# Attention probabilities transposed in 32x32 blocks on the vector engine instead of on the matmul engine, in an adaLN + attention + GRU + FFN kernel

## The reference

```python
# x: (B=128, S=32, E=256); 32 heads of 8 features
y    = adaln(x)                      # block summary attention, then a layer norm per token
q, k, v = split(y @ W_attn + b_attn)         # (128, 32 heads, 32, 8)
scores = einsum('bhqd,bhkd->bhqk', q, k) / sqrt(8)
scores = where(causal, scores, -10000) + alibi
probs  = softmax(scores, axis=-1)            # (128, 32, 32, 32)
attn   = einsum('bhqk,bhkd->bhqd', probs, v)
x      = x + attn @ W_proj + b_proj
h      = GRU over the 32 tokens of x, state (128, 256)   # sequential
out    = x + h @ (weight * scale).T + bias
```

## Time and profile before

| | us |
|---|---|
| median of 3 runs | 445.61 (443.76 to 445.76) |
| the profiled execution, its own time | 445.15 |
| its span, first to last instruction | 443.3 |
| start, up to the first `normalise` | 51.29 |
| attention, first to last `normalise` | 205.76 |
| the rest: last projection, GRU, FFN | 186.25 |

### The profile page before, as it was taken

One profiled execution on the slowest core, in us unless ns is written; L12 is line 12 of the kernel. 1 busy time (PEld: TensorE's weight loads), 2 busy tenths in 40 slices (PEclk: granted clock), 3 DMA queues, 4 the chain that ended last, 5 costly groups with the idle time before them and its releaser, 6 DMA issues.

```text
span 443.3 us, 13432 instructions
## 1 busy us (share of the span) xinstructions
PE 423.8 (96%) x5448; PEld 350.9 (79%) x5448; DVE 326.1 (74%) x995; ACT 236.4 (53%) x553; POOL 93.2 (21%) x114
## 2 busy tenths in 40 slices
PE   8899999999999999999999899999999999999994
PEld 5656687786877878778687698899999999999984
DVE  3587888798888877879777844677776677777665
ACT  7355657566575675755666753444444444444341
POOL 7663142432132221322235500000000000000000
PEclk9999999999999999999999999999999999999999
DMA  7942413223133141231213000001000000000001
GB/s 289 394 183 70 135 40 100 70 61 109 35 90 96 50 120 39 86 95 53 74 33 92 27 1 2 0 2 47 20 31 24 25 24 26 25 24 25 24 25 71
DMA packets 34268, 30.36 MB, mean 68 GB/s; under 512 B 4128, under 2 KB 29344, under 8 KB 34208
## 3 DMA queue, kind: packets, MB, share of 16 engines
q1 hardware_dynamic: 34208, 29.51, 20.5%
HBM read 16.92 MB, written 8.39 MB: 57 GB/s over the span
## 4 chain that ended last, share of the span: by engine, by line
PE 75%; DVE 15%; ACT 4%; issue 3%; POOL 1%; DVEq 0%; ACTq 0%; POOLq 0%
PE ps_a L1267 10%; PE ps_s L1432 7%; PE ps_t L1432 6%; PE ps_o L1432 6%; PE ps_s L1327 6%; PE ps_s L1488 5%; PE ps_t L1488 5%; PE ps_a L1488 4%; PE ps_t L1340 4%; PE ps_m L1371 4%; PE ps_m L1488 4%; PE ps_o L1351 3%; PE ps_m L1363 3%; DVE mx L963 2%; ACT y L599 2%
## 5 line engine op out<-in xcount | busy, mean ns | idle before, releaser
L531 POOL TENSOR_TENSOR sc<-masked,mx 128x512 f32<-128x512 f32 x32 | 45.7, 1429 | 143.3 <-DVE mx L963 143.3
L955 DVE COPY_PREDICATED masked<-kst,ps_s 128x512 f32<-128x512 int32 x64 | 44.1, 736 | 6.1 <-PE ps_s L1327 5.8
L1267 PE MATMUL ps_a<-yT_r,w_qkv_r 128*128 128x512 f32 x180 | 46.0, 403 | 1.3 <-DVE yT_r L936 0.9
L754 ACT ACTIVATE zg<-ps_t,brz 128x128 f32<-128x128 f32 x64 | 20.1, 365 | 39.6 <-PE ps_t L1432 37.3
L963 DVE TENSOR_REDUCE mx<-masked 128x16 f32<-128x512 f32 x64 | 40.5, 674 | 0.0
L1267 PEld LDWEIGHTS ps_a<-yT_r,w_qkv_r 128*128 128x128 f32 x180 | 32.6, 188 | 9.6 <-issue 2.8
L637 ACT ACTIVATE sc<-sc 128x512 f32<-128x512 f32 x64 | 37.3, 621 | 4.2 <-DVE sc L969 2.9
L1101 DVE SCALAR_TENSOR_TENSOR rg<-ps_o,vec,rg 128x128 f32<-128x128 f32 x64 | 19.5, 346 | 24.8 <-PE ps_o L1432 23.8
L570 ACT ACTIVATE pT<-ps_t 128x512 f32<-128x512 f32 x64 | 34.9, 595 | 4.5 <-PE ps_t L1340 3.4
L1327 PE MATMUL ps_s<-kbd,qn 64*32 64x256 f32 x1024 | 36.3, 382 | 0.8 <-issue 0.8
L1432 PEld LDWEIGHTS ps_s<-hT,w_hh 128*128 128x128 f32 x256 | 33.1, 191 | 4.9 <-DVE hT L1119 2.8
(11 more groups left out here) (159 smaller groups left out, 827.2 us busy)
## 6 DMA issues: line engine op xcount, KB each, us to landing
xf<-in_x_feat SPq DMA_DIRECT2D x8, 512.0 KB, 9.5
xg<-in_x_tok SPq DMA_DIRECT2D x8, 512.0 KB, 5.1
kbd<-kn SPq DMA_DIRECT2D x128, 32.0 KB, 1.9
v_dram<-vn SPq DMA_DIRECT2D x16, 256.0 KB, 2.5
vbd<-v_dram SPq DMA_DIRECT2D x64, 64.0 KB, 2.1
out_feat<-ost SPq DMA_DIRECT2D x16, 256.0 KB, 2.0
w_qkv<-in_wqkv SPq DMA_DIRECT2D x1, 768.0 KB, 9.7
w_ih<-in_wih SPq DMA_DIRECT2D x1, 768.0 KB, 13.3
```

Of the source, the lines that this page charges most:

```text
L531: nc.gpsimd.tensor_tensor(shifted, kept, m.unsqueeze(2).to_broadcast([P, NH // 2, S]), ALU.subtract).then_inc(sc_sub[1], 1)
L754: nc.scalar.activation(dst[:, c, :], gate_part(gate, c, t), ACT.Sigmoid, bias=brz[:, b0 + c:b0 + c + 1]).then_inc(done, 1)
L955: nc.vector.copy_predicated(kept, keep.unsqueeze(1).to_broadcast([P, NH // 2, S]), ps_s[:, h * 512:(h + 1) * 512].rearrange("p (h k) -> p ...
L1267: last = nc.tensor.matmul(bank, w_qkv_r[a][:, c, first_col + m * P:first_col + (m + 1) * P], yT_r[b][:, c, :], start=(a == b == c == 0), s ...
```

## The change

The scores of a tile are laid out with head-in-four and query down the partitions, and sequence, head-quad and key along the free dimension. Then every 32x32 block [query x key] can be transposed where it stands, and DVE does so with two instructions of 128x512, SBUF to SBUF. The eight PE transposes and the two ACT copies of a tile are gone. The rest follows from it: 

- `scores` is 32 products of 32 rows and 32 columns of the array with 128 moving columns, where it was 16 of 64 rows with 256; its semaphore rises once per tile, so `softmax_mask` waits for all of a tile's scores. The row of the array and the output quadrant are rotated against each other, `head = (r + c) % HG`.
- `kbd` has two buffers in the same memory (4 key slots in place of 8), 4 DMAs for each half group with twice the bytes each.
- `transpose_probs(n)` moves to DVE, after `softmax_mask(n+1)` and ahead of `softmax_max(n+1)`.
- The residual sum of all tiles but the last goes to POOL, with ACT's `projection_out` in front of it.
- ACT runs `softmax_exp(n)` at the start of step n, on both sides of `attn_out(n-1)`, in place of at the end of step n-1, and `projection_out(n-1)` right behind it, ahead of the copies of keys, queries and values and of `normalise_tokens`.
- On DVE `rest_of_y` goes ahead of `softmax_mask`, `token_stats` behind `softmax_shift`.
- `ps_t`, free now, takes the queries and values; `ps_a` keeps the keys and the transposed tokens.

```diff
-BY_POOL = range(NT - GT, NT - 1)
+BY_POOL = range(NT - 1)
@@ memory
-            kbd = ...nc.sbuf_tensor("kbd", [P, C, KH, GC], F32))
+            kbd = ...nc.sbuf_tensor("kbd", [P, 2, C, KH, GC], F32))
-            pT = ...nc.sbuf_tensor("pT", [P, NQ, P], F32))
+            pT = ...nc.sbuf_tensor("pT", [P, NH * S], F32))
@@ ACT tile_step
+                softmax_exp(n, n % 2, 0)
                 if i == 0 and not last_group:
                     round_y(g + 1, 0)
                     round_y(g + 1, 1)
                 if n > 0:
                     attn_out(n - 1)
-                probs_out(n)
+                softmax_exp(n, n % 2, 1)
+                if n - 1 in BY_POOL:
+                    projection_out(n - 1)
...
-                if n - 1 in BY_POOL:
-                    projection_out(n - 1)
-                if n + 1 < NT:
-                    softmax_exp(n + 1, (n + 1) % 2)
@@ DVE
-                    dve.wait_ge(sc_mm, 2 * n + h + 1)
+                    dve.wait_ge(sc_mm, n + 1)
...
+            def transpose_probs(n, p):
+                dve.wait_ge(pv_mm, n)
+                for h in range(2):
+                    cols = slice(h * 512, (h + 1) * 512)
+                    dve.wait_ge(sc_exp, 2 * n + h + 1)
+                    nc.vector.transpose(pT[:, cols], sc[:, p, cols]).then_inc(pt_out, 1)
@@ DVE tile_step
+                if i == 0 and g + 1 < NG:
+                    rest_of_y(g + 1)
                 if n + 1 < NT:
                     softmax_mask(n + 1, (n + 1) % 2)
-                if i == 0 and g + 1 < NG:
-                    rest_of_y(g + 1)
                 if norm_ahead and i == 2:
                     add_proj(g + 2, ps_a)
...
+                transpose_probs(n, n % 2)
...
-                if norm_ahead and i == 2:
-                    token_stats(g + 2)
                 if n + 1 < NT:
                     softmax_max(n + 1, (n + 1) % 2)
                     softmax_shift(n + 1, (n + 1) % 2)
+                if norm_ahead and i == 2:
+                    token_stats(g + 2)
@@ PE
-                for c in range(C):
-                    for r in range(RH):
-                        rows = slice(r * P // RH, (r + 1) * P // RH)
-                        for b in range(TB):
...
-                            last = nc.tensor.matmul(ps_s[b * S:(b + 1) * S, out_cols], qn[rows, g % 2, c, cols],
-                                                    kbd[rows, c, :, cols], start=True, stop=True,
-                                                    tile_position=(r * P // RH, b * S))
+                for b in range(TB):
+                    cols = slice(i * P + b * S, i * P + (b + 1) * S)
+                    for c in range(C):
+                        out_col = score_column(c * KH, b)
+                        for r in range(HG):
+                            rows, head = slice(r * S, (r + 1) * S), (r + c) % HG
+                            last = nc.tensor.matmul(
+                                ps_s[head * S:(head + 1) * S, out_col:out_col + KH * S], qn[rows, g % 2, c, cols],
+                                kbd[rows, g % 2, c, :, cols], start=True, stop=True,
+                                tile_position=(r * S, head * S))
+                last.then_inc(sc_mm, 1)
@@ PE tile_step
-                transpose_probs(n, n % 2, first=(n == 0))
```

More of the change, by code:

```diff
@@ L26 @@
 HG = 4
-RH = 2
-KH = P // RH // 8
 NQ = NH // HG
-HW = NQ // 2
+KH = NQ // C
 GC = GT * P
@@ L307, in product_bank, with value_bank @@
                     4: ps_s[:, 512:1024], 5: ps_m[:, :]}.get(k, ps_a[:, 0:512])
+        def value_bank(k, h):
+            return (ps_m[:, :], ps_a[:, 0:512])[h] if k == 0 else ps_t[:, h * 512:(h + 1) * 512]
         def block_keys(k):
@@ L378, in load_k @@
                 cols = slice(half * TH * P, (half + 1) * TH * P)
-                for h in range(KH):
-                    sp.dma_start(kbd[h:P:KH, :, h, cols], kn[h:P:KH, :, cols]).then_inc(k_in[half], DMA)
+                for j in range(KH):
+                    sp.dma_start(kbd[j:P:KH, k % 2, :, j, cols], kn[j:P:KH, :, cols]).then_inc(k_in[half], DMA)
             def save_v(k, half):
@@ L556, in _ @@
                         softmax_shift(n + 1)
+                    if i == 2 and g + 2 < NG:
+                        inverse_std(g + 2)
                     if n - 1 in BY_POOL:
@@ L560, in _ @@
                         block_sums(g + EARLY)
-                    if i == 2 and g + 2 < NG:
-                        inverse_std(g + 2)
                     if g == NG - 2 and i > 0:
@@ L610, in q_chunk @@
                 if m == 0 and k >= 2:
-                    act.wait_ge(sc_mm, 2 * GT * (k - 1))
-                nc.scalar.activation(qn[:, k % 2, m, :], ps_a[:, m * GC:(m + 1) * GC], ACT.Identity,
+                    act.wait_ge(sc_mm, GT * (k - 1))
+                nc.scalar.activation(qn[:, k % 2, m, :], ps_t[:, m * GC:(m + 1) * GC], ACT.Identity,
                                      bias=bq[:, m:m + 1], scale=SCALE).then_inc(q_out, 1)
@@ L629, in v_half, with softmax_exp @@
                 nc.scalar.activation(vn[:, half, :, :].rearrange("p h (t w) -> p t h w", t=TH),
-                                     ps_a[:, half * 512:(half + 1) * 512].rearrange("p (t h w) -> p t h w", t=TH, h=HG),
+                                     value_bank(k, half).rearrange("p (t h w) -> p t h w", t=TH, h=HG),
                                      ACT.Identity, scale=key_factor).then_inc(v_out, 1)
[L633 to L644, removed]
+            def softmax_exp(n, p, h):
+                act.wait_ge(sc_sub[h], n + 1)
+                part = sc[:, p, h * 512:(h + 1) * 512]
+                nc.scalar.activation(part, part, ACT.Exp).then_inc(sc_exp, 1)
             def projection_out(n):
@@ L1066, in tile_step @@
                     cond_scores(3)
+                if i == 0 and g in (0, 2):
+                    cond_shift(2 + g // 2)
+                transpose_probs(n, n % 2)
                 if i == 1 and g in (0, 2):
@@ L1075, in tile_step @@
                     softmax_shift(n + 1, (n + 1) % 2)
-                if i == 0 and g in (0, 2):
-                    cond_shift(2 + g // 2)
+                if norm_ahead and i == 2:
+                    token_stats(g + 2)
                 if norm_ahead and i == 2:
@@ L1260, in project_qk @@
             def project_qk(k, first_col, done, m):
-                bank = ps_a[:, m * GC:(m + 1) * GC]
+                bank = (ps_a if done is k_mm else ps_t)[:, m * GC:(m + 1) * GC]
                 for a, b in ((0, 0), (1, 0), (0, 1)):
@@ L1320, in scores, with prob_block @@
                     pe.wait_ge(sc_out, 2 * n)
[L1321 to L1341 removed]
+                for b in range(TB):
[9 more added lines that the diff above has]
+                last.then_inc(sc_mm, 1)
+            def prob_block(q, b):
+                return slice(score_column(q, b), score_column(q, b) + S)
             def probs_v(n, g, i):
@@ L1598, in qk_cols @@
     def qk_cols(w):
-        return w.reshape(-1, RH, C, KH, HD).transpose(0, 2, 1, 4, 3).reshape(-1, E)
+        split = w.reshape(-1, C, KH, HG, HD)
+        rows = [np.roll(split[:, c], -c, axis=2).transpose(0, 2, 3, 1).reshape(-1, P) for c in range(C)]
+        return np.concatenate(rows, 1)
     def v_cols(w):
```

66 lines of the change are left out of this document (29 added, 37 removed).

## The result

The kernel after takes 457.54 us in the median of 4 runs (455.98 to 458.38), the kernel before 445.65 beside it. The ratio is 1.0273, with a 95% interval of 1.0233 to 1.0313: slower, as forecast, but by 12 us where the sum gave 4. The profiled execution took 455.98 us, 10.83 more than that of before.

The account below looks back on a forecast made before the run. PE was taken to limit steps i = 0 and 1, DVE i = 2, i = 3 and three steps of the last group. Terms summed to +4.15 us on 445.15, giving 449.3 us; range 440 to 468.

Parts of the forecast that it names:

- the pace of DVE's transposes: Two DVE transposes per tile: 1.27 us a pair, net +0.60 per step where DVE is the limit.
- the scores' eight parts: PE's scores: eight array parts work at once, 0.8 us plus 0.25 of start-up, costed at nothing.
- the wait for ACT ahead of `project_out`: `project_out` follows `transpose_attn` by 0.90 us, not 1.15, so PE's steps gain 0.25, not 1.05.
- i = 2 and i = 3 as DVE's steps: DVE limits them: i = 2 +0.88 in groups 0 to 5, i = 3 +0.60 in groups 2 to 6.
- POOL's sums hidden: Two residual sums on POOL, about 1.0 us a tile, cost nothing; POOL is busy 1.41 to 2.62 of a step.
- Both transpose rivals: DVE transposes fast, 0.43 us each: 442.0 us, chance 0.20; or slow, 2.6 a pair: 472.1, chance 0.12.
- both scores rivals: Scores four at a time: 465.3 us, chance 0.12; row parts sharing a bank take turns: 497.3, chance 0.04.
- i = 0, "-0.25 - 0.34 + 0.09": Groups 1 to 6: shorter `project_out` wait, keys no longer late, tokens 0.09 later; -0.50 each, -3.0 us in all.
- i = 3 in groups 0 and 1, "PE stays the limit: -0.25": PE's block products of 1.9 us keep PE the limit there; -0.25 each, -0.5 us in all.
- i = 1, -0.25: PE's step gains 0.25 us and nothing else moves; in 7 groups -1.75 us.
- The start, -1.2: First step: `rest_of_y` ahead of the mask, no PE transposes, first scores ahead of half the values; -1.2 us.
- The fourth step's zero: Last group's fourth step: 0.8 us saved by the copy, as much lost by the order; zero.

Follow-up runs that it names:

- the kernel with filler in one step: Kernel after, with PE transposing the identity into free `ps_t`, result unread, in steps i = 3 of groups 0 to 6 alone: 453.43 us, ratio 1.0185.
- the tokens first: Kernel after with ACT's `normalise_tokens` and `cond_out` ahead of `projection_out` for i = 3: 455.36 us, ratio 1.0217.
- the two best kernels: Kernel after with `normalise_tokens` and `cond_out` earlier, both shifts on POOL, idle PE products throughout (442.83 us) or in i = 3 of groups 0 to 6 alone (442.89).

## Why the prediction was right in direction and wrong in size

*Right:* the pace of DVE's transposes; the scores' eight parts; the wait for ACT ahead of `project_out`; i = 2 and i = 3 as DVE's steps (+0.71 and +0.37 a step, forecast 0.88 and 0.60); POOL's sums hidden; the GRU unchanged (186.22 us). Both transpose rivals and both scores rivals are out: four parts writing one bank, in different quadrants, would have taken 3.2 us if they took turns, and took 1.15. The rule that I had from the Trainium skill, TensorEngine Tiling (Array Packing), Gotcha 1, and gave a chance doesn't hold for this use.

*Wrong:* the measured sum is 6.8 us over mine. Of these 2.8 come by the clock; 1.9 by the program's supply (1.2 in one pair of steps, 0.7 in i = 1); 2.3 in the pairs i = 3 and i = 0 that start in groups 0 and 1 (13.86 and 15.20 us, +0.21 and +0.63 where I had -0.75 each); 0.4 in the rest of i = 1; 0.9 at the start; less 1.0 in i = 2 and 0.6 in the last group. What failed most was never written as a term: that PE's own pace stays what it was.

- **The clock.** I priced PE's idle time in i = 3 and in the fourth step of the last group at nothing, since DVE or a chain sets those steps. The granted clock fell there and in the last group: it is slow in the second half of i = 3 and at the start of i = 0 (158 to 162 and 189 to 192 us), and in the fourth step. By the windows: pairs i = 3 and i = 0 at groups 3 to 4 and 4 to 5, 13.92 and 13.56 us where the kernel with filler in one step has 13.03 and 13.01, and the fourth step at 5.40 where 4.03 is had at full clock: 0.89 + 0.55 + 1.37 = 2.8 us.
- **The program's supply.** The pair at groups 2 to 3 holds both stalls: 14.23 us, against 13.03 without them, 1.2. Two more are too short to show as idle time: the scores that start at 199.69 and 228.55 us take 1.43 and 1.49 us, not 1.15, with a halt behind matmuls 3499 and 4130, 12 and 17 times 126.2 past 1984. Their steps i = 1 take 7.60 and 6.97 us, 7.30 and 6.61 with filler in one step: 0.7. Against that, the kernel before has its own stall at groups 5 to 6 (13.49 us for the pair, else 12.7); it is gone after (13.02). That gives 0.6 back by luck, as much as the three other pairs are too long beside clock and supply (0.2 each). Whether the change brings more such stalls because it gives PE twice as many matmuls for the scores is not shown. Filler in one step takes 4.1 us off the median (457.54 to 453.43; 3.9 by the ratios). I can't split that further by medians, as the filler moves the packets too.
- **i = 0, "-0.25 - 0.34 + 0.09".** The arithmetic held: tokens done at 5.56, so scores 0.75 later, at 6.31 us after the start of i = 3; measured at full clock, in the kernel with filler in one step, 4.93 + 1.35 = 6.28. But I added this -0.50 to a +0.60 for i = 3 as if the two were apart. The pair is one chain, bound through ACT; DVE's share of it is free. At full clock it is 13.0, my two terms gave 12.9, and the +0.37 in place of +0.60 for i = 3 is lost again in i = 0. (It is +0.37 since a pair of transposes takes 1.21 us from start to start, not 1.27, and the normalising and the mask ahead of it take 0.13 less than before. In i = 2 the mask starts only 0.08 later, not 0.21.)
- **i = 3 in groups 0 and 1, "PE stays the limit: -0.25".** Two things stood behind. `cond_out`, the copy of the block products, comes after `normalise_tokens` on ACT; its PSUM is what `transpose_y` writes next, and PE stands idle for 0.75 us ahead of that (72.66 and 102.06; the copy ends 0.09 and 0.10 before). With the tokens first that wait is gone, and i = 0 of group 1 takes 7.70, not 8.45 us. And in group 1 DVE scales `w_f` in this step, which I overlooked; DVE's and POOL's timelines after:

```profile
100.87 1.54 DVE L1043 TENSOR_TENSOR w_f<-w_f,row 128x512 f32<-128x512 f32 x1
102.33 0.48 DVE L1045 TENSOR_TENSOR brz<-vec 128x4 f32<-128x4 f32 x1
```

```profile
100.44 1.43 POOL L533 TENSOR_TENSOR sc<-masked,mx 128x512 f32<-128x512 f32 x1 [1.69 <-DVE mx L956]
101.83 1.46 POOL L541 TENSOR_TENSOR xf<-xo,xf 128x128 f32<-128x128 f32 x2
```

  It took 0.85 us before, with POOL idle but for its first 0.3, and takes 1.54 now; POOL's pair of sums is stretched too, 1.46 for 1.01. The Trainium skill, SBUF — State Buffer, section "SBUF: two separate sides", has DVE operations with two SBUF inputs and POOL's take turns at one port pair. The trace agrees. So does the kernel with both shifts on POOL, where DVE no longer does one beside it: POOL's shift takes 1.06 us there, 1.43 in the kernel after.
- **i = 1, -0.25.** Steady steps without a stall gained 0.07: `transpose_attn` starts 0.05 later behind the longer scores, and queries follow `project_out` after 0.91, not 0.81. That row was there to be read: at the last tile the same eight matmuls took 1.16, not 1.06. A matmul group that starts on an idle PE costs 0.1 more.
- **The start, -1.2.** -0.34 in the profiled execution. The `normalise` that ends it came between 50.1 and 53.3 us in kernels that differ little there, so the term is within its own scatter.
- The fourth step's zero held but for the clock: 4.03 us at full clock, 4.04 before.

Of the rivals, none was what happened; a clock that falls in steps in which the change leaves PE less to do was not among them. The direction came out right, but 4.7 of the 10.9 us lost, by the clock and the supply, were in no term of the sum.

## What to carry to other kernels

Work taken off PE has two prices that no busy share shows: PE's clock can fall in the step that it leaves empty, and then the next step, which is PE's, pays; and PE can stand still for its own program in the midst of small matmuls, at places that move with every matmul added ahead of them. Look at the granted clock beside PE's busy time in each window of a version before believing a sum, and try a few idle products in the emptiest step, as these alone gave 4 us here (clock and supply together). Look for such stalls in the kernel before as well. And price neighbouring steps as one chain, by what the second waits for: 0.6 us less for DVE in i = 3 were worth 0.0 for the pair, one swap on ACT 1.1.

## What was not expected of the hardware

- In the start of the kernel with forty products more, PE's records leave no gap (busy 12.73 of 12.73 us) and the granted clock was 0.68 all the same; the row after it in the same answer, 26.60 to 40.00, has 0.66:

```profile
13.87:26.60 12.73, 12.73 (x82) 12.71 (x80) 0.74 (x1) 0.00 (x0) 1.49 (x3) 0.68 0.96 366
```

  The 80 records have 8 columns each behind a 128x128 weight load. The clock was 1.00 up to 18 us, with 11 of them in a microsecond, and 0.50 from 19, with 6 to 7; in the mean they took 0.16 us apiece, some 13 us where I had counted on next to nothing.
- The clock's fall differs from one execution to the next: the four runs of the kernel after have mean clocks of 0.983, 0.979, 0.976 and 0.964 and take 455.98, 457.07, 458.01 and 458.38 us, in this order.
- Where PE's program comes in packets, it waited up to 1.63 us for one.
- Whether the two best kernels (442.83 and 442.89 us) gain by the block transposes themselves is open: without them, POOL's sums alone gave 444.14, and no run put PE's transposes beside the other edits.
